# Weights of the first half in pairs of members, the later wait carried by the instruction, and two duties moved between engines

## The chip, the cores and the metric

The kernel runs on one core of a Trainium2 chip. TensorE (PE in the profile) multiplies matrices out of SBUF into PSUM, VectorE (DVE) and ScalarE (ACT) work elementwise, GpSimd (POOL) clears small tensors and issues gathers, and SyncE (SP) issues most of the transfers (DMAs). Each engine takes its own instructions in the order in which they are written; between engines there are only semaphores. The metric is the device time of one execution in microseconds. The kernel before takes 80.88 us, the median of three runs of 80.46, 80.88 and 80.88.

## The reference

```
w = weights[conditions]                       # x: 32 batches of 32 x 256, one 32 x 32 table entry per batch
y = einsum('bct,bcd->bdt', x, w)              # mixing
h = silu(y @ w_gate) * (y @ w_up)             # 256 -> 1024
h_sparse = keep the 2 largest |h| of every 4 neighbours, else 0
out = x + h_sparse @ w_down                   # 1024 -> 256
```

All numbers are 32-bit floats. The kernel gets their accuracy out of faster matmuls by dividing each operand into a high part (rounded) and a low part (what the rounding left), and adding three products: high by high, low by high, high by low.

## The kernel before

The 1024 rows of y are two halves of 512 (half 0 and 1). The 1024 columns of the gate and up matrices are two halves as well (q = 0 and 1), each of four members j = 0 to 3 of 128 columns: member j holds the columns that are j-th in their group of four, so the choice of 2 in 4 is elementwise among four tiles. A pair n is one gate product and one up product of 128 by 512 for one (half, q, j); there are 16 pairs, in the order half, q, j. Each product is 6 matmuls (three terms, two halves k of the 256 inputs). PSUM banks for pairs go round in threes.

The start, which the change touches, goes as follows. SP (L173 to L176) loads the condition numbers, x of half 0, and the k = 0 part of the q = 0 gate weights. POOL clears the tensor `warm` (L199) and marks blocks in `own_block` (L200 to L203). PE multiplies `warm` by itself 12 times (L520) while nothing else can be done. When the condition numbers are there, VectorE adds row numbers (L439), POOL gathers the table rows (L206), VectorE transposes them (L351) and spreads them on diagonals (L359); then PE mixes (L529 for k = 0, L543 for k = 1). ScalarE and VectorE divide each result y and each piece of the weights into high and low: ScalarE writes the high part (L233 weights, L237 y), VectorE subtracts it for the low part (L366 weights, L373 y). A piece of weights is one entry of the list `PIECES`; the semaphores `w_hi` and `w_lo` count pieces whose high and low part is there, `y_hi` and `y_lo` the same for y.

PE then computes the gates of pairs 0 and 1 side by side (`first_gates`, L570, 12 matmuls that alternate between the two pairs: for each k the terms high-high, low-high, high-low), after them the up products of pairs 0 and 1 (L558), pair 2, the mixing of half 1 (L543), and the pairs 3 to 15 (L558). Last come 102 matmuls by `w_down` (L600), the addition of x (L435) and six outputs, stored by SP (L194), the last of them by ScalarE's queue (L335).

An instruction can wait for several semaphores. The built program gives the wait that is written first to the instruction itself; those written after it become one instruction of their own ahead of it, which only waits. In the listings below, the last name in a bracket is the wait that the instruction carries, and the names ahead of it are those of the separate waiting instruction.

Of the kernel before, what the change touches and what calls it, by code (L numbers as in the profile page):

```python
# [5 lines left out]
NQ = 2  # L6
M = 4
# [3 lines left out]
def adaln_ffn(nc: bass.Bass, x: bass.AP, x_t: bass.AP, cond: bass.AP, table: bass.AP,  # L11
# [5 lines left out]
    f32 = mybir.dt.float32  # L17
    f32r = mybir.dt.float32r
    bf16 = mybir.dt.bfloat16
    ALU = mybir.AluOpType  # L20
# [27 lines left out]
    with ctx:  # L48
# [39 lines left out]
        y_banks = banks[:, 6:6 + KT]  # L88

        cond_in = sem("cond_in")  # L90
        x_in = [sem(f"x_in{i}") for i in range(NH)]
        w_in = [[None, sem("gate_in1")], [sem(f"up_in{q}") for q in range(NQ)]]
        first_in = [sem(f"first_in{k}") for k in range(KT)]
# [45 lines left out]
        def split_y(part, half, k, end):  # L139
# [6 lines left out]

        PIECES = [(0, w, k, k + 1) for w in range(2) for k in range(KT)] + \
                 [(q, w, 0, KT) for q in range(1, NQ) for w in range(2)]

        def pieces_until(q, w, k):  # L150
            return 1 + max(i for i, piece in enumerate(PIECES) if piece[:2] == (q, w) and piece[2] <= k)

        GATE_PIECES_END = PIECES.index((1, 0, 0, KT)) + 1

# [3 lines left out]
                   (1, 1, 0, TH // 2, gate_bank(PAIRS - 1)), (1, 1, TH // 2, TH, up_bank(PAIRS - 1))]  # L158
        UNFINISHED = 3
        HALVED = range(2, M)  # L160
# [5 lines left out]

        def raw_piece(q, w, k, end):

            return raw_w[w][:, q, k:end].rearrange("p k (j g) -> p k j g", j=M)

        @block.sync
        def _(sp):
            sp.dma_start(cond_sb[:], cond).then_inc(cond_in, 16)  # L173

            sp.dma_start(x_sb[:, 0:GH, :], x[0]).then_inc(x_in[0], 16)
            sp.dma_start(raw_w[0][:, 0, 0], w_gate[0, 0]).then_inc(first_in[0], 16)  # L176

            sp.wait_ge(mix_in[0], 16)
            for k in range(1, KT):
                sp.dma_start(raw_w[0][:, 0, k], w_gate[0, k]).then_inc(first_in[k], 16)  # L180
            sp.dma_start(raw_w[1][:, 0], w_up[0]).then_inc(w_in[1][0], 16)
            sp.wait_ge(w_in[1][0], 16)
            sp.dma_start(x_sb[:, GH:NG, :], x[1]).then_inc(x_in[1], 16)
            sp.dma_start(raw_w[0][:, 1], w_gate[1].rearrange("k p n -> p k n")).then_inc(w_in[0][1], 16)
            sp.dma_start(raw_w[1][:, 1], w_up[1]).then_inc(w_in[1][1], 16)
            sp.dma_start(down_raw[:], w_down).then_inc(down_in, 16)
            sp.wait_ge(w_hi, GATE_PIECES_END)
            sp.wait_ge(w_lo, GATE_PIECES_END)
            sp.dma_start(xt_sb, x_t).then_inc(xt_in, 16)
            for i, (half, k, begin, end, _) in enumerate(OUTPUTS[:-1]):  # L190
                if i != UNFINISHED:
                    cols = slice(half * TH + begin, half * TH + end)
                    sp.wait_ge(out_done, i + 1)
                    sp.dma_start(out[:, k, cols], xt_sb[:, k, cols]).then_inc(stored, 16)  # L194
            sp.wait_ge(stored, 16 * (len(OUTPUTS) - 1))

        @block.gpsimd
        def _(pool):
            nc.gpsimd.memset(warm[:], 0.0).then_inc(warm_zero, 1)  # L199
            nc.gpsimd.memset(own_block[:], 0.0).then_inc(blocks_marked, 1)  # L200
            pool.wait_ge(blocks_marked, 1)
            for b in range(NB):
                nc.gpsimd.memset(own_block[b * C:(b + 1) * C, b:b + 1], 1.0).then_inc(blocks_marked, 1)  # L203
            pool.wait_ge(rows_done, 1)
            for half in range(NH):
                nc.gpsimd.indirect_dma_start(  # L206
                    out=mix_row[:, half], out_offset=None, in_=table,
                    in_offset=bass.IndirectOffsetOnAxis(ap=rows_sb[:, half:half + 1], axis=0),
                    engine_sem=gather_sent,
                ).then_inc(mix_in[half], 16)  # L210

            def low_down(q):
                pool.wait_ge(down_neg, q + 1)
                pool.dma_start(down_hl[:, LO, q].rearrange("p j t -> p (j t)"), down_raw[:, q],  # L214
                               accum_op=ALU.add).then_inc(down_lo_sent[q], 16)

            def low_h(u, j, end):
                pool.wait_ge(h_neg, parts_until(u, j))
                pool.dma_start(h_hl[:, u, LO, j:end], hs[u][:, j:end],  # L219
                               accum_op=ALU.add).then_inc(h_lo_sent[u][j // 2], 16)  # L220

            low_down(0)
            low_down(1)
            for u in range(SENT):
                for j, end in PARTS[u]:
                    low_h(u, j, end)

        @block.scalar
        def _(act):

            def high_weights(q, w, k, end):
                act.wait_ge(first_in[k] if (q, w) == (0, 0) else w_in[w][q], 16)
                nc.scalar.activation(w_hl[w][:, HI, q, k:end], raw_piece(q, w, k, end), ACT.Copy).then_inc(w_hi, 1)  # L233

# [38 lines left out]
            for k in range(KT):  # L273
                high_weights(*PIECES[k])
                high_y(*Y_PIECES[k])
            for piece in PIECES[KT:2 * KT]:
                high_weights(*piece)
            act.wait_ge(table_loaded, 1)
            gate_silu(0)
            gate_silu(1)  # L280
            absolute(0)
            high_weights(*PIECES[4])
            gate_silu(2)
            absolute(1)
            high_weights(*PIECES[5])
            high_y(*Y_PIECES[KT])
# [44 lines left out]
            high_h(3, 3, 4)  # L331
            half, k, begin, end, _ = OUTPUTS[-1]
            cols = slice(half * TH + begin, half * TH + end)
            act.wait_ge(out_done, len(OUTPUTS))
            act.dma_start(out[:, k, cols], xt_sb[:, k, cols]).then_inc(stored, 16)  # L335

        @block.vector
        def _(dve):
# [23 lines left out]
            def low_weights(i):  # L362
                q, w, k, end = PIECES[i]
                dve.wait_ge(first_in[k] if (q, w) == (0, 0) else w_in[w][q], 16)
                dve.wait_ge(w_hi, i + 1)
                nc.vector.tensor_tensor(w_hl[w][:, LO, q, k:end], raw_piece(q, w, k, end),  # L366
                                        w_hl[w][:, HI, q, k:end].bitcast(f32), ALU.subtract).then_inc(w_lo, 1)

            def low_y(i):
                half, k, end = Y_PIECES[i]  # L370
                dve.wait_ge(mixed, KT * half + end)
                dve.wait_ge(y_hi, i + 1)
                nc.vector.tensor_tensor(split_y(LO, half, k, end), mixed_y(half, k, end),  # L373
                                        split_y(HI, half, k, end).bitcast(f32), ALU.subtract).then_inc(y_lo, 1)
# [54 lines left out]
            def output(i):  # L429
# [3 lines left out]
                if i > UNFINISHED:  # L433
                    dve.wait_ge(out_done, UNFINISHED + 1)
                nc.vector.tensor_tensor(xt_sb[:, k, cols], bank[:, begin:end], xt_sb[:, k, cols],  # L435
                                        ALU.add).then_inc(out_done, 1)

            dve.wait_ge(cond_in, 16)
            nc.vector.tensor_tensor(rows_sb[:], cond_sb[:, 0:NH], cond_sb[:, NH:2 * NH], ALU.add).then_inc(rows_done, 1)  # L439
            dve.wait_ge(blocks_marked, 1 + NB)  # L440
            transpose_rows(0)
            diagonal(SPANS[0])
            diagonal(SPANS[1])
            for k in range(KT):
                low_weights(k)
                low_y(k)
            for i in range(KT, 2 * KT):
                low_weights(i)
# [3 lines left out]
            diagonal(SPANS[2])  # L452
            low_weights(4)
            product(2)
            compare(0, 1)
            low_weights(5)
            low_y(KT)
# [59 lines left out]
        def _(pe):  # L517
# [4 lines left out]
            def mixing_by_batch():  # L522

                pe.wait_ge(x_in[0], 16)
                pe.wait_ge(transposed, 1)
                for g in range(GH):
# [22 lines left out]
            def split_product(dst, w, q, half, j):  # L549

                terms = [(s, m, k) for s, ms in ((HI, (HI, LO)), (LO, (HI,))) for k in range(KT) for m in ms]
                for i, (s, m, k) in enumerate(terms):

                    if half == 0 and j == 0:
                        pe.wait_ge(w_hi if s == HI else w_lo, pieces_until(q, w, k))
                    if q == 0 and j == 0:
# [5 lines left out]
            def first_gates():  # L562

                terms = [(s, m, k) for k in range(KT) for s, m in ((HI, HI), (LO, HI), (HI, LO))]
                for i, (s, m, k) in enumerate(terms):
                    if i > 0:
                        pe.wait_ge(w_hi if s == HI else w_lo, pieces_until(0, 0, k))
                    pe.wait_ge(y_hi if m == HI else y_lo, k + 1)
                    for n in (0, 1):
                        nc.tensor.matmul(gate_bank(n), w_hl[0][:, s, 0, k, n], y_hl[:, m, 0, k],  # L570
                                         start=i == 0, stop=i == len(terms) - 1)
# [35 lines left out]
            warm_up(WARM_START)  # L607
            pe.wait_ge(w_hi, pieces_until(0, 0, 0))
            mixing_by_batch()
# [64 lines left out]
```

## Time and profile before

| | us |
|---|---|
| runs | 80.46, 80.88, 80.88 (median 80.88) |
| profiled execution | 80.44 |
| its span, first to last instruction | 78.6 |
| busy: PE, PE weight loads, DVE, ACT, POOL | 74.5, 59.5, 62.1, 41.7, 8.6 |

The profile shows one execution; its span leaves 1.84 us of that execution's time outside. PE is busy for 95% of the span, so the time is PE's work, what stands ahead of it and behind it, and the short stretches in which PE's instructions do not follow each other at their own pace. Of a busy time on PE one should know that the end of a matmul is modelled; what counts is the distance from the start of one to the start of the next. The views below are the chain that ended last, tables of stretches (`--windows`: busy time and number of instructions of each engine, granted clock, share of the 16 DMA engines, GB/s) and timelines.

### The profile page before, as it was taken

What the parts mean: (1) busy time and instruction counts of PE and PEld (TensorE: products, weight loads), DVE (VectorE), ACT (ScalarE), POOL (GpSimd) and SP (SyncE); (2) the same over time, 40 slices, a digit from 0 to 9 for tenths busy, and PEclk for the clock granted to TensorE, in tenths of its full rate; (3) what the DMA queues carried; (4) which work ended last, traced back from release to release, by engine and by line L of the source; (5) the groups of instructions that cost most, each with busy time, mean ns of one, the idle gap of its engine ahead of it and who ended that gap; (6) DMA issues with size and microseconds to landing.
All of it is one profiled execution on the core that took longest, in us unless ns stands there. A gap on an engine that the chain in (4) does not pass through costs nothing.

```text
span 78.6 us, 1020 instructions
## 1 busy us (share of the span) xinstructions
PE 74.5 (95%) x362; PEld 59.5 (76%) x362; DVE 62.1 (79%) x91; ACT 41.7 (53%) x61; POOL 8.6 (11%) x18
## 2 busy tenths in 40 slices
PE   3999999999999999999999999999999999999950
PEld 1338778888888888888888888888888888888840
DVE  0017691699879999599999979999999999994460
ACT  6122753869453375599897769789380402730000
POOL 5550000000000013000713000006200000000000
PEclk9999999999999999999999999999999999999999
DMA  0857559984900004900099990003995000003333
GB/s 1 250 183 201 232 154 381 413 377 92 425 33 0 0 0 79 188 0 0 15 194 200 194 198 13 4 0 60 200 177 96 0 0 0 8 0 138 137 142 118
DMA packets 3221, 9.64 MB, mean 123 GB/s; under 512 B 496, under 2 KB 752, under 8 KB 2960
## 3 DMA queue, kind: packets, MB, share of 16 engines
q0 software_dynamic: 928, 3.28, 21.9%
q1 hardware_dynamic: 2144, 6.16, 21.8%
q10 hardware_dynamic: 144, 0.13, 0.5%
q8 instruction: 3, 0.05, 0.2%
q14 instruction: 2, 0.02, 0.1%
HBM read 5.38 MB, written 1.05 MB: 82 GB/s over the span
## 4 chain that ended last, share of the span: by engine, by line
PE 95%; POOL 1%; DVE 1%; issue 0%; POOLq 0%
PE banks L558 52%; PE banks L600 28%; PE banks L520 6%; PE banks L543 4%; PE banks L570 4%; PE banks L529 1%; POOL warm L199 1%; DVE gate_raw L435 1%; POOLq L663 0%
## 5 line engine op out<-in xcount | busy, mean ns | idle before, releaser
L558 PE MATMUL banks<-y_hl,up_hl 128*128 128x512 f32 x96 | 24.2, 389 | 0.0
L600 PE MATMUL banks<-h_hl,down_hl 128*128 128x512 f32 (+1 forms) x102 | 22.0, 376 | 0.0
L558 PE MATMUL banks<-y_hl,gate_hl 128*128 128x512 f32 x84 | 21.4, 390 | 0.0
L600 PEld LDWEIGHTS banks<-h_hl,down_hl 128*128 128x128 f32 x102 | 18.5, 188 | 3.6
L558 PEld LDWEIGHTS banks<-y_hl,up_hl 128*128 128x128 f32 x96 | 18.0, 188 | 3.8
L558 PEld LDWEIGHTS banks<-y_hl,gate_hl 128*128 128x128 f32 x84 | 15.7, 188 | 3.2
L243 ACT ACTIVATE silu<-banks 128x512 f32<-128x512 f32 x16 | 9.6, 597 | 12.4 <-PE banks L558 12.1
L384 DVE TENSOR_TENSOR h<-banks,silu 128x512 f32<-128x512 f32 x12 | 8.3, 689 | 4.4 <-ACT silu L243 4.4
L264 ACT ACTIVATE h_hl<-h 128x1024 fp32r<-128x1024 f32 (+1 forms) x8 | 6.7, 843 | 3.9 <-DVE h L420 3.9
L420 DVE SCALAR_TENSOR_TENSOR h<-count,h 128x512 f32<-128x512 bf16 x12 | 7.9, 687 | 0.1
L520 PE MATMUL banks<-warm 128*128 128x512 bf16 x12 | 4.8, 586 | 1.3 <-POOL warm L199 1.3
L250 ACT ACTIVATE x_sb<-h 128x512 f32<-128x512 f32 x8 | 4.9, 626 | 1.7 <-DVE h L384 1.7
L435 DVE TENSOR_TENSOR gate_raw<-banks,gate_raw 128x512 f32<-128x512 f32 (+1 forms) x6 | 3.5, 602 | 2.4 <-PE banks L600 2.3
L214 POOL DMA_DIRECT2D down_hl<-down_raw x2 | 1.8, 919 | 31.5 <-ACT down_hl L259 31.5
L219 POOL DMA_DIRECT2D h_hl<-h x4 | 3.7, 928 | 13.4 <-ACT h_hl L268 13.4
L395 DVE TENSOR_TENSOR far<-x_sb 128x1024 bf16<-128x1024 f32 x4 | 4.9, 1222 | 0.2
L395 DVE TENSOR_TENSOR far<-a_even 128x1024 bf16<-128x1024 f32 x4 | 4.9, 1220 | 0.2
L520 PEld LDWEIGHTS banks<-warm 128*128 128x128 bf16 x12 | 1.6, 141 | 4.1 <-issue 2.7
L268 ACT ACTIVATE h_hl<-h 128x1024 fp32r<-128x1024 f32 x4 | 4.2, 1054 | 0.0
L233 ACT ACTIVATE gate_hl<-gate_raw 128x512 fp32r<-128x512 f32 (+1 forms) x3 | 2.3, 771 | 3.6 <-DMA gate_raw<-in_w_gate 3.6
L264 ACT ACTIVATE h_hl<-up_raw 128x1024 fp32r<-128x1024 f32 x2 | 2.1, 1054 | 3.2 <-DVE up_raw L420 3.2
L351 DVE STREAM_TRANSPOSE h<-h 128x128 f32<-128x128 f32 x2 | 0.8, 406 | 3.1 <-DMA h<-in_table,rows_sb 3.1
(39 smaller groups left out, 68.1 us busy)
## 6 DMA issues: line engine op xcount, KB each, us to landing
h_hl<-h POOLq DMA_DIRECT2D x4, 512.0 KB, 6.1
x_sb<-in_x SPq DMA_DIRECT2D x2, 512.0 KB, 3.4
up_raw<-in_w_up SPq DMA_DIRECT2D x2, 512.0 KB, 4.7
down_raw<-in_w_down SPq DMA_DIRECT2D x1, 1024.0 KB, 7.8
gate_raw<-in_x_t SPq DMA_DIRECT2D x1, 1024.0 KB, 4.8
down_hl<-down_raw POOLq DMA_DIRECT2D x2, 512.0 KB, 5.0
out<-gate_raw SPq DMA_DIRECT2D x3, 256.0 KB, 2.4
gate_raw<-in_w_gate SPq DMA_DIRECT2D x2, 256.0 KB, 3.3
```

The costliest lines, as they stand in the source:

```text
L219: pool.dma_start(h_hl[:, u, LO, j:end], hs[u][:, j:end], accum_op=ALU.add).then_inc(h_lo_sent[u][j // 2], 16)
L243: nc.scalar.activation(silu[:, n % 3], gate_bank(n), ACT.Silu).then_inc(silu_done, 1)
L250: nc.scalar.activation(a[u % 2][:, j], hs[u][:, j], ACT.Abs).then_inc(abs_done, 1)
L264: nc.scalar.activation(h_hl[:, u, HI, j:end], hs[u][:, j:end], ACT.Copy).then_inc(h_hi, 1)
L268: nc.scalar.activation(h_hl[:, u, LO, j:end], hs[u][:, j:end], ACT.Copy, scale=-1.0).then_inc(h_neg, 1)
L384: nc.vector.tensor_tensor(hs[u][:, j], up_bank(n), silu[:, n % 3], ALU.mult).then_inc(h_done, 1)
L395: step(nc.vector.tensor_tensor(far[:, j - 2::2], au[:, 0:2], au[:, j:j + 1].broadcast_to([P, 2, TH]), ALU.is_ge))
L420: nc.vector.scalar_tensor_tensor(hs[u][:, j], count[:, j], bound, hs[u][:, j], op, ALU.mult).then_inc(masked, 1)
L435: nc.vector.tensor_tensor(xt_sb[:, k, cols], bank[:, begin:end], xt_sb[:, k, cols], ALU.add).then_inc(out_done, 1)
L520: nc.tensor.matmul(gate_bank(0), warm[:, 0:P], warm[:], start=True, stop=True)
L558: last = nc.tensor.matmul(dst, w_hl[w][:, s, q, k, j], y_hl[:, m, half, k], start=i == 0, stop=i == len(terms) - 1)
L600: last = nc.tensor.matmul(bank[:, begin:end], down_hl[:, s, q, j, k * P:(k + 1) * P], h_hl[:, u, m, j, begin:end], start=(q, j, m, s) == f ...
```

## The change

The q = 0 gate and up weights are no longer divided into pieces by k with all four members, but by pairs of members: the pieces are now gate k = 0 and gate k = 1 of members 0 and 1, up of members 0 and 1 (both k), then gate and up of members 2 and 3 (both k). The weights lie in HBM by pairs of members accordingly, so a partition's contiguous run in these transfers is 1 KB; the q = 1 weights come in two transfers each. Pair 2 waits for the new later pieces. Further, `warm` is cleared by VectorE; at many places the order in which two waits are written is exchanged; and the last of the six outputs is stored by SP, the one before it by ScalarE's queue.

```
+        PIECES = [(0, 0, k, k + 1, 0, 2) for k in range(KT)] + [(0, 1, 0, KT, 0, 2)] + \
+                 [(0, w, 0, KT, 2, M) for w in range(2)] + [(1, w, 0, KT, 0, M) for w in range(2)]
+        LATER = KT + 3
...
-        PIECES = [(0, w, k, k + 1) for w in range(2) for k in range(KT)] + \
-                 [(q, w, 0, KT) for q in range(1, NQ) for w in range(2)]
...
-        UNFINISHED = 3
+        UNFINISHED, LEFT = 3, 4
...
-            sp.dma_start(raw_w[0][:, 0, 0], w_gate[0, 0]).then_inc(first_in[0], 16)
+            sp.dma_start(raw_w[0][:, 0, 0, 0:2 * P], w_gate[0, 0, 0]).then_inc(first_in[0], 16)
 
             sp.wait_ge(mix_in[0], 16)
             for k in range(1, KT):
-                sp.dma_start(raw_w[0][:, 0, k], w_gate[0, k]).then_inc(first_in[k], 16)
-            sp.dma_start(raw_w[1][:, 0], w_up[0]).then_inc(w_in[1][0], 16)
-            sp.wait_ge(w_in[1][0], 16)
+                sp.dma_start(raw_w[0][:, 0, k, 0:2 * P], w_gate[0, 0, k]).then_inc(first_in[k], 16)
+            sp.dma_start(raw_w[1][:, 0, :, 0:2 * P], w_up[0, 0].rearrange("k p n -> p k n")).then_inc(up_in, 16)
+            for w, weights in enumerate((w_gate, w_up)):
+                sp.dma_start(raw_w[w][:, 0, :, 2 * P:4 * P],
+                             weights[0, 1].rearrange("k p n -> p k n")).then_inc(rest_in[w], 16)
+            sp.wait_ge(up_in, 16)
             sp.dma_start(x_sb[:, GH:NG, :], x[1]).then_inc(x_in[1], 16)
-            sp.dma_start(raw_w[0][:, 1], w_gate[1].rearrange("k p n -> p k n")).then_inc(w_in[0][1], 16)
-            sp.dma_start(raw_w[1][:, 1], w_up[1]).then_inc(w_in[1][1], 16)
+            for w, weights in enumerate((w_gate, w_up)):
+                for i in range(2):
+                    sp.dma_start(raw_w[w][:, 1, :, 2 * i * P:2 * (i + 1) * P],
+                                 weights[1, i].rearrange("k p n -> p k n")).then_inc(second_in[w], 16)
...
-            for i, (half, k, begin, end, _) in enumerate(OUTPUTS[:-1]):
-                if i != UNFINISHED:
+            for i, (half, k, begin, end, _) in enumerate(OUTPUTS):
+                if i not in (UNFINISHED, LEFT):
...
-            nc.gpsimd.memset(warm[:], 0.0).then_inc(warm_zero, 1)
             nc.gpsimd.memset(own_block[:], 0.0).then_inc(blocks_marked, 1)
...
-            half, k, begin, end, _ = OUTPUTS[-1]
+            half, k, begin, end, _ = OUTPUTS[LEFT]
...
+            nc.vector.memset(warm[:], 0.0).then_inc(warm_zero, 1)
             dve.wait_ge(cond_in, 16)
+            dve.wait_ge(blocks_marked, 1 + NB)
             nc.vector.tensor_tensor(rows_sb[:], cond_sb[:, 0:NH], cond_sb[:, NH:2 * NH], ALU.add).then_inc(rows_done, 1)
-            dve.wait_ge(blocks_marked, 1 + NB)
...
-                pe.wait_ge(x_in[0], 16)
                 pe.wait_ge(transposed, 1)
+                pe.wait_ge(x_in[0], 16)
...
-                    if half == 0 and j == 0:
-                        pe.wait_ge(w_hi if s == HI else w_lo, pieces_until(q, w, k))
+                    if half == 0 and (j == 0 or (q, j) == (0, 2)):
+                        pe.wait_ge(w_hi if s == HI else w_lo, pieces_until(q, w, k, j))
...
                 for i, (s, m, k) in enumerate(terms):
+                    pe.wait_ge(y_hi if m == HI else y_lo, k + 1)
                     if i > 0:
-                        pe.wait_ge(w_hi if s == HI else w_lo, pieces_until(0, 0, k))
-                    pe.wait_ge(y_hi if m == HI else y_lo, k + 1)
+                        pe.wait_ge(w_hi if s == HI else w_lo, pieces_until(0, 0, k, 0))
```

VectorE's first instructions in the kernel before, from the row numbers to the low parts of the q = 0 weights; `h` is the tensor in which the gathered and transposed table rows lie, `mix_in0` the arrival of the gather:

```order
L439 ISA rows_sb<-cond_sb 128x4 [waits cond_in]
L351 STREAM_TRANSPOSE h<-h 128x4x32 [waits mix_in0,blocks_marked]
L359 TENSOR_TENSOR h<-h,own_block 128x256 [waits transposed] x2
L366 TENSOR_TENSOR gate_hl<-gate_raw,gate_hl 128x512 [waits w_hi,first_in0]
L373 TENSOR_TENSOR y_hl<-banks,y_hl 128x512 [waits y_hi,mixed]
L366 TENSOR_TENSOR gate_hl<-gate_raw,gate_hl 128x512 [waits w_hi,first_in1]
L373 TENSOR_TENSOR y_hl<-banks,y_hl 128x512 [waits y_hi,mixed]
L366 TENSOR_TENSOR up_hl<-up_raw,up_hl 128x512 [waits w_hi,up_in0] x2
```

The same place in the changed kernel:

```order
L458 MEMSET warm 128x256
L461 ISA rows_sb<-cond_sb 128x4 [waits blocks_marked,cond_in]
L372 STREAM_TRANSPOSE h<-h 128x4x32 [waits mix_in0]
L380 TENSOR_TENSOR h<-h,own_block 128x256 [waits transposed] x2
L386 TENSOR_TENSOR gate_hl<-gate_raw,gate_hl 128x256 [waits first_in0,w_hi]
L393 TENSOR_TENSOR y_hl<-banks,y_hl 128x512 [waits mixed,y_hi]
L386 TENSOR_TENSOR gate_hl<-gate_raw,gate_hl 128x256 [waits first_in1,w_hi]
L393 TENSOR_TENSOR y_hl<-banks,y_hl 128x512 [waits mixed,y_hi]
L386 TENSOR_TENSOR up_hl<-up_raw,up_hl 128x2x256 [waits up_in,w_hi]
L386 TENSOR_TENSOR gate_hl<-gate_raw,gate_hl 128x2x256 [waits rest_in0,w_hi]
L386 TENSOR_TENSOR up_hl<-up_raw,up_hl 128x2x256 [waits rest_in1,w_hi]
```

The clearing of `warm` stands first; the transpose carries its only wait itself; the wait for ScalarE's high part (`w_hi`, `y_hi`) is now the one that each subtraction carries; the two gate pieces ahead of the y pieces are half as wide, and three pieces of 512 follow where two stood.

SP's transfers at the start of the kernel before:

```order
L175 DMA x_sb<-in_x 128x1024
L176 DMA gate_raw<-in_w_gate 128x512
L180 DMA gate_raw<-in_w_gate 128x512 [waits mix_in0]
L181 DMA up_raw<-in_w_up 128x1024
L183 DMA x_sb<-in_x 128x1024 [waits up_in0]
L184 DMA gate_raw<-in_w_gate 128x2x512
L185 DMA up_raw<-in_w_up 128x1024
L186 DMA down_raw<-in_w_down 128x2048
```

And in the changed kernel:

```order
L192 DMA x_sb<-in_x 128x1024
L193 DMA gate_raw<-in_w_gate 128x256
L197 DMA gate_raw<-in_w_gate 128x256 [waits mix_in0]
L198 DMA up_raw<-in_w_up 128x2x256
L200 DMA gate_raw<-in_w_gate 128x2x256
L200 DMA up_raw<-in_w_up 128x2x256
L203 DMA x_sb<-in_x 128x1024 [waits up_in]
L206 DMA gate_raw<-in_w_gate 128x2x256 x2
L206 DMA up_raw<-in_w_up 128x2x256 x2
L208 DMA down_raw<-in_w_down 128x2048
```

Ahead of SP's wait for the up weights stand four transfers instead of two; behind it six instead of four.

## Rows read from the trace of the kernel before

**Rows 1.** Chain that ended last: start us, us, what.
```profile
1.33 4.83 PE banks L520 x12
6.24 1.09 PE banks L529 x32
...
8.42 2.91 PE banks L570 x12
11.33 5.46 PE banks L558 x24
...
18.65 35.40 PE banks L558 x156
...
75.91 0.42 DVE gate_raw L435
```
**Rows 2.** Stretches: us, busy PE, PEld, DVE, ACT, POOL (count), PEclk, DMA, GB/s.
```profile
6.00:9.25 3.25, 3.17 (x46) 2.82 (x46) 2.23 (x6) 1.41 (x3) 0.00 (x0) 1.00 0.81 262
8.18:11.17 2.99, 2.99 (x16) 2.20 (x14) 2.60 (x5) 2.27 (x4) 0.00 (x0) 1.00 0.42 145
11.17:13.91 2.74, 2.74 (x14) 2.25 (x12) 0.99 (x2) 0.60 (x1) 0.00 (x0) 1.00 1.05 381
```
**Rows 3.** Timeline of the start: us, us, engine, line, operation, idle before.
```profile
0.75 0.52 POOL L199 MEMSET warm<- 128x512 bf16 x1 [0.29 <-POOLq L663]
...
2.41 0.16 DVE L439 CUSTOM_DVE_ANT_0 rows_sb<-cond_sb 128x4 uint16<-128x4 uint16 x1 [2.41 <-DMA cond_sb<-in_cond]
...
5.57 0.10 PEld L520 LDWEIGHTS banks<-warm 128*128 128x128 bf16 x1 [0.27 <-issue]
...
5.68 0.41 DVE L351 STREAM_TRANSPOSE h<-h 128x128 f32<-128x128 f32 x1 [3.11 <-DMA h<-in_table,rows_sb]
...
6.21 1.01 PEld L529 LDWEIGHTS banks<-h,x_sb 32*128 32x128 f32 x32 [0.54 <-ACT gate_hl L233]
...
7.39 0.60 ACT L237 ACTIVATE y_hl<-banks 128x512 fp32r<-128x512 f32 x1 [1.39 <-PE banks L529]
...
8.09 0.69 DVE L373 TENSOR_TENSOR y_hl<-banks,y_hl 128x512 fp32r<-128x512 f32 x1 [0.60 <-ACT y_hl L237]
...
8.44 0.63 ACT L233 ACTIVATE gate_hl<-gate_raw 128x512 fp32r<-128x512 f32 x1 [0.45 <-DMA gate_raw<-in_w_gate]
...
8.97 0.58 ACT L237 ACTIVATE y_hl<-banks 128x512 fp32r<-128x512 f32 x1
...
9.67 1.15 ACT L233 ACTIVATE up_hl<-up_raw 128x512 fp32r<-128x512 f32 x2
...
9.67 1.23 PEld L570 LDWEIGHTS banks<-y_hl,gate_hl 128*128 128x128 f32 x6 [0.29 <-issue]
...
12.81 0.60 ACT L243 ACTIVATE silu<-banks 128x512 f32<-128x512 f32 x1 [1.99 <-PE banks L558]
...
13.44 0.69 DVE L384 TENSOR_TENSOR h<-banks,silu 128x512 f32<-128x512 f32 x1 [1.75 <-ACT silu L243]
```
**Rows 4.** Last warm-up matmul, then PE's starts after 8.7 us (timeline, PE).
```profile
5.78 0.38 PE L520 MATMUL banks<-warm 128*128 128x512 bf16 x1
8.72 1.09 PE L570 MATMUL banks<-y_hl,gate_hl 128*128 128x512 f32 x4
```
**Rows 5.** Arrival of the two gathers after issue.
```profile
DMA to landing us min/median/max: 2.6/2.6/2.7
```
**Rows 6.** Transfers: KB each, median us from issue to landing.
```profile
out<-gate_raw SPq DMA_DIRECT2D x1, 128.0 KB, 1.9
out<-gate_raw ACTq DMA_DIRECT2D x1, 128.0 KB, 1.9
```
**Rows 7.** Timeline of the end.
```profile
74.48 1.22 DVE L435 TENSOR_TENSOR gate_raw<-banks,gate_raw 128x512 f32<-128x512 f32 x2 [0.67 <-PE banks L600]
...
75.73 0.33 SPq L194 DMA_DIRECT2D out<-gate_raw  x1
...
76.37 0.37 ACTq L335 DMA_DIRECT2D out<-gate_raw  x1
```

More of the change, by code:

```diff
@@ L88, in adaln_ffn, with pieces_until, source @@
         y_banks = banks[:, 6:6 + KT]
+        PIECES = [(0, 0, k, k + 1, 0, 2) for k in range(KT)] + [(0, 1, 0, KT, 0, 2)] + \
+                 [(0, w, 0, KT, 2, M) for w in range(2)] + [(1, w, 0, KT, 0, M) for w in range(2)]
+        LATER = KT + 3
+        def pieces_until(q, w, k, j):
+            return 1 + max(i for i, p in enumerate(PIECES) if p[:2] == (q, w) and p[2] <= k < p[3] and p[4] <= j < p[5])
+        def source(i):
+            q, w, k, _, j, _ = PIECES[i]
+            if q == 1:
+                return second_in[w], 32
+            if j == 2:
+                return rest_in[w], 16
+            return (first_in[k], 16) if w == 0 else (up_in, 16)
         cond_in = sem("cond_in")
         x_in = [sem(f"x_in{i}") for i in range(NH)]
-        w_in = [[None, sem("gate_in1")], [sem(f"up_in{q}") for q in range(NQ)]]
+        up_in = sem("up_in")
+        rest_in = [sem(f"rest_in{w}") for w in range(2)]
+        second_in = [sem(f"second_in{w}") for w in range(2)]
         first_in = [sem(f"first_in{k}") for k in range(KT)]
@@ L145, in adaln_ffn @@
         SPANS = [slice(0, 2), slice(2, 4), slice(4, 8)]
-        PIECES = [(0, w, k, k + 1) for w in range(2) for k in range(KT)] + \
-                 [(q, w, 0, KT) for q in range(1, NQ) for w in range(2)]
-        def pieces_until(q, w, k):
-            return 1 + max(i for i, piece in enumerate(PIECES) if piece[:2] == (q, w) and piece[2] <= k)
-        GATE_PIECES_END = PIECES.index((1, 0, 0, KT)) + 1
+        GATE_PIECES_END = PIECES.index((1, 0, 0, KT, 0, M)) + 1
         OUTPUTS = [(0, 0, 0, TH, y_banks[:, 0]), (0, 1, 0, TH, y_banks[:, 1]),
@@ L165, in parts_until, with raw_piece, split_piece @@
             return sum(len(p) for p in PARTS[:u]) + 1 + max(i for i, p in enumerate(PARTS[u]) if p[0] <= j)
-        def raw_piece(q, w, k, end):
-            return raw_w[w][:, q, k:end].rearrange("p k (j g) -> p k j g", j=M)
+        def raw_piece(i):
+            q, w, k, end, j, j_end = PIECES[i]
+            return raw_w[w][:, q, k:end].rearrange("p k (j g) -> p k j g", j=M)[:, :, j:j_end]
+        def split_piece(i, part):
+            q, w, k, end, j, j_end = PIECES[i]
+            return w_hl[w][:, part, q, k:end, j:j_end]
         @block.sync
@@ L229, in _, with high_weights @@
         def _(act):
-            def high_weights(q, w, k, end):
-                act.wait_ge(first_in[k] if (q, w) == (0, 0) else w_in[w][q], 16)
-                nc.scalar.activation(w_hl[w][:, HI, q, k:end], raw_piece(q, w, k, end), ACT.Copy).then_inc(w_hi, 1)
+            def high_weights(i):
+                act.wait_ge(*source(i))
+                nc.scalar.activation(split_piece(i, HI), raw_piece(i), ACT.Copy).then_inc(w_hi, 1)
             def high_y(half, k, end):
@@ L273, in _ @@
             for k in range(KT):
-                high_weights(*PIECES[k])
+                high_weights(k)
                 high_y(*Y_PIECES[k])
-            for piece in PIECES[KT:2 * KT]:
-                high_weights(*piece)
+            for i in range(KT, LATER):
+                high_weights(i)
             act.wait_ge(table_loaded, 1)
@@ L281, in _ @@
             absolute(0)
-            high_weights(*PIECES[4])
+            high_weights(LATER)
             gate_silu(2)
             absolute(1)
-            high_weights(*PIECES[5])
+            high_weights(LATER + 1)
             high_y(*Y_PIECES[KT])
@@ L362, in low_weights @@
             def low_weights(i):
-                q, w, k, end = PIECES[i]
-                dve.wait_ge(first_in[k] if (q, w) == (0, 0) else w_in[w][q], 16)
                 dve.wait_ge(w_hi, i + 1)
-                nc.vector.tensor_tensor(w_hl[w][:, LO, q, k:end], raw_piece(q, w, k, end),
-                                        w_hl[w][:, HI, q, k:end].bitcast(f32), ALU.subtract).then_inc(w_lo, 1)
+                dve.wait_ge(*source(i))
+                nc.vector.tensor_tensor(split_piece(i, LO), raw_piece(i),
+                                        split_piece(i, HI).bitcast(f32), ALU.subtract).then_inc(w_lo, 1)
             def low_y(i):
                 half, k, end = Y_PIECES[i]
+                dve.wait_ge(y_hi, i + 1)
                 dve.wait_ge(mixed, KT * half + end)
-                dve.wait_ge(y_hi, i + 1)
                 nc.vector.tensor_tensor(split_y(LO, half, k, end), mixed_y(half, k, end),
@@ L446, in _ @@
                 low_y(k)
-            for i in range(KT, 2 * KT):
+            for i in range(KT, LATER):
                 low_weights(i)
@@ L452, in _ @@
             diagonal(SPANS[2])
-            low_weights(4)
+            low_weights(LATER)
             product(2)
             compare(0, 1)
-            low_weights(5)
+            low_weights(LATER + 1)
             low_y(KT)
@@ L522, in mixing_by_batch @@
             def mixing_by_batch():
+                pe.wait_ge(transposed, 1)
                 pe.wait_ge(x_in[0], 16)
-                pe.wait_ge(transposed, 1)
                 for g in range(GH):
@@ L607, in _ @@
             warm_up(WARM_START)
-            pe.wait_ge(w_hi, pieces_until(0, 0, 0))
+            pe.wait_ge(w_hi, pieces_until(0, 0, 0, 0))
             mixing_by_batch()
@@ L649, in columns @@
         w = _np.asarray(w).reshape(T // P, P, NQ, P, M)
-        return w.transpose(2, 1, 0, 4, 3).reshape(NQ, P, T // P, M * P)
+        return w.transpose(2, 4, 0, 1, 3).reshape(NQ, 2, M // 2, T // P, P, P).transpose(0, 1, 3, 4, 2, 5).reshape(
+            NQ, 2, T // P, P, -1)
     down = _np.asarray(inputs["L0_ffn_w_down"]).reshape(NQ, P, M * T).transpose(1, 0, 2)
@@ L657 @@
         "table": table,
-        "w_gate": columns(inputs["L0_ffn_w_gate"]).transpose(0, 2, 1, 3),
+        "w_gate": columns(inputs["L0_ffn_w_gate"]),
         "w_up": columns(inputs["L0_ffn_w_up"]),
```

2 lines of the change are left out of this document (1 added, 1 removed).

## The prediction, made before the changed kernel was run

> **What bounds the kernel now.** I read the chain that ended last first, because with PE busy for 95% of the span the question is which stretches of PE are not run at its own pace. The chain is PE from 1.33 us on, and VectorE and a store at the end [rows 1]. From 11.33 us PE runs at 5.46 / 24 = 0.2275 us per matmul of 512 columns, and the 156 after 18.65 us at 35.40 / 156 = 0.227. Nothing there waits, so no wait that goes there can pay. Three places are left: what stands ahead of the mixing at 6.24, the first gates, and the end behind PE.
>
> Ahead of the mixing the timeline [rows 3] shows what was late. The gather wakes the transpose at 5.68; it ends at 6.09; PE's first weight load for the mixing starts at 6.21, 0.12 later. The page blames ScalarE's gate piece for that wait, but the transpose ended last of what the rows show. The twelve warm-up matmuls were just over. The weights of the twelfth were loaded at 5.57, when the eleventh starts, and (5.57 - 1.33) / 10 = 0.424 is the lower level of the clock (512 columns at 1.2 GHz are 0.427); the twelfth starts at 5.78 [rows 4], 0.21 later, which is the higher level. At that pace it gives PE free at 5.99, 0.22 before the load. The column of the granted clock reads 1.00 throughout [rows 2], so the level is read from the spacing alone.
>
> The first gates are 12 matmuls from 8.18 to 11.17, 2.99 us; the next 12 take 2.74 [rows 2]. So 0.25 us are lost. The third matmul starts at 8.72 [rows 4] instead of 8.18 + 2 x 0.228 = 8.64: 0.08 is lost there, just behind the wait for the first y. The rest, 0.17, is lost around 9.67, where the weight load had been idle for 0.29 and starts 0.12 after ScalarE's second y (8.97 + 0.58 = 9.55) [rows 3]. That y is late because ScalarE was at the k = 1 gate piece from 8.44 to 9.07, and that piece was late because its 256 KB were.
>
> **The change part by part.** The sum is made against the profiled execution's 80.44 us, 0.5% below the median of 80.88.
>
> Order of waits. Hand-overs of both kinds stand in the trace. Where the late wait is carried by a waiting instruction of its own, VectorE starts 0.10 after ScalarE's end (7.39 + 0.60 = 7.99 to 8.09). Where the instruction carries it, 0.03 (12.81 + 0.60 = 13.41 to 13.44) [rows 3]. So one exchange is worth 0.07 where it is on the path. On the path is the transpose, whose wait for the gather the instruction now carries: -0.07, of which I take 0.06, since this releaser is a transfer. PE's own first load keeps the transpose in the separate wait, because the w_hi wait is still written first: 0. The row addition gets a second wait, for the marked blocks, but the marking has no duty at 2.41 us and moves earlier with POOL's 0.52 us of clearing gone: 0. VectorE's subtractions for y and weights get 0.07 each; those of y feed the third term of each k, hidden behind the first two: 0 on their own.
>
> Less traffic ahead of the gather. The first gate transfer is 128 KB instead of 256. The two gathers arrive 2.6 and 2.7 us after issue [rows 5], the second after the x and first gate transfers have ended. So this is worth 0 to 0.1; I take 0.05, the middle, because the rows do not say which of the two gathers is the late one.
>
> The half as wide gate pieces. The 0.17 around 9.67 goes if the second y is ready 0.2 us earlier. With 256 columns for 512, the k = 1 high part costs between 0.32 (half of 0.63) and 0.63. If the transfer came no earlier than before, it would run from 8.44 to 8.76 at best, and y from there to 9.37: 0.18 earlier. The transfer has half its bytes; at the mean rate of that stretch, 262 GB/s [rows 2], 131 kB are 0.5 us. Then ScalarE goes to the piece straight from the first y (7.93 in the new times), ends by 8.56 even at the full 0.63, and the second y is there by about 9.0 to 9.2. The stall is gone then: -0.17, bounds -0.08 (no earlier arrival) and -0.25 (all of the loss). The 0.08 behind the first y stays, since nothing there changes.
>
> Warm-up cleared by VectorE. POOL needs 0.52 from 0.75 on [rows 3]. VectorE's clearing of 128 x 256 is not in the trace; the nearest rows are 0.16 (128 x 4) and 0.69 (128 x 512). So the warm-up starts between 0.17 later and 0.36 earlier; I take half of the 0.69 for half the width, 0.35, so 0.17 earlier. In this execution that is worth nothing: PE was free 0.22 before the transpose let it go, which covers the later case as well but for 0.01 to 0.02. It has a price only where PE is not free by then, which is the second case below.
>
> Rest pieces and more transfers. Members 2 and 3 add a transfer and a piece each for gate and up. Pair 2 needs them 12 matmuls after the first gates, near 13.7; I expect the transfers by about 10 to 11 and the divisions, 0.6 to 0.7 each, by 12.5. ScalarE idled 1.99 before 12.81 [rows 3], which is the cover. SP issues two transfers more before its wait for the up weights, but that wait ends earlier with half the bytes: 0. The Trainium skill, page "DMA: Bandwidth & Descriptors", section "Bandwidth", speaks against this edit: it wants transfers batched to 1 MiB or more. By that rule the pieces of 128 and 256 KB would lose rate. The rows have 262 GB/s over pieces of 256 and 512 KB; what slower ones would do is the last case below.
>
> Last store. ScalarE's queue issued it 0.04 after VectorE's end (75.91 + 0.42 = 76.33 to 76.37), SP issued the one before 0.03 after (75.70 to 75.73) [rows 1, 7], and both kinds take 1.9 us [rows 6]: 0, bounds -0.05 and +0.05.
>
> Sum: -0.06 - 0.05 - 0.17 = -0.28. PE's later stages move as a block, since ScalarE and VectorE follow PE there. 80.44 - 0.28 = 80.16, a factor of 0.9965; on the median, 80.88 x 0.9965 = 80.60. By the bounds of its terms (0 to -0.07, 0 to -0.10, -0.08 to -0.25, and 0.05 either way for the store) the change is worth -0.03 to -0.47 in this execution, 80.41 to 80.85 on the median.
>
> **The rivals.**
>
> More than the profile shows. The shown runs lie at 80.46 and at 80.88, and the profiled one at 80.44 is of the quicker kind. If in the others the clock rises later, the warm-up's last matmuls run at 0.427 each and PE is not free until 1.33 + 12 x 0.427 = 6.45, 0.24 after the transpose. There the earlier start of the warm-up pays its 0.17 of that 0.24, beside the 0.28: 80.88 - 0.45 = 80.43, and less if the mixing too leaves the lower level earlier. For it: two of three runs lie 0.42 higher, and 0.24 plus some mixing at the lower level would make that. Against it: no row shows such a run. The Trainium skill, page "TensorE: Matmul & The Clock Gate", says that the moment of the rise differs by half a microsecond between runs of one kernel; no run shown here can confirm it. With 5.57 moved by that much it would be this case by estimate.
>
> It does not do what it says. If the transfer of the k = 1 gates is ruled by its fixed time and not by its bytes, and the gather does not come earlier, then only 0.06 to 0.14 is left: about 80.8.
>
> Slower by the transfers. Four transfers of 1 KB runs must land before ScalarE can go on to the first silu, at 12.81 - 0.28 = 12.53. The last of them, the up weights of members 2 and 3, must be there 0.63 earlier, at 11.9. From 6.0 on they and the second gather are 983 kB; with some 0.6 for arrival (the row of 6.00 to 9.25 ends its bytes there, and the up weights were used at 9.67 after a landing just before) this needs 983 kB / 5.3 us = 185 GB/s, against 262 so far. If runs of 1 KB halve the rate to 131, the last bytes come at 13.5 and the piece at 14.1, 2.2 late. Silu 0, silu 1 and the diagonals of half 1 follow in order on ScalarE and VectorE. I count half of the 2.2 as hidden, because silu 1 itself came 1.3 after silu 0 and only then the diagonals: +1.1 - 0.28 = +0.8, 81.7. Against it: the change halves a partition's run for the gates and quarters it for the up weights, and less than a third of the rate may go before anything waits.
>
> **How the numbers follow.** The forecast 0.48, more than that 0.34, no effect 0.10, slower transfers 0.08. A measurement of this kernel tells no change from about 0.5%, 0.40 us. Of the forecast 0.15 lies beyond that, of the second case 0.9, of the third none: faster 0.07 + 0.31 = 0.38. Slower: the last case and 0.01 for what nobody saw, 0.09. The rest, 0.53, is within. The range 80.0 to 81.1 holds the first three cases, with 0.4 below the second for what the mixing may gain, and leaves out most of the last.
>
> **What would show it.** PE's first mixing load at about 6.1 instead of 6.21; the transpose 0.03 to 0.07 after the gather; ScalarE's k = 1 gate piece right behind the first y, at about 7.9; no idle weight load near 9.5; 12 first gates in about 2.8 us; the tail behind PE unchanged; PE at 0.227 per matmul from then on. It would be wrong if PE waits at pair 2 or at the mixing of half 1, if the k = 1 gates land at 8.4 as before, or if the mixing runs at the lower level after a longer idle of PE.

## The result, and the profile after

Six runs of the changed kernel took 80.18 to 80.35 us, median 80.21; six of the kernel before, beside them, 80.46 to 80.88, median 80.75. The ratio is 0.9943, with a 95% interval of 0.992 to 0.9967. A second comparison, of twelve runs against 33, gave 0.9965 (0.9949 to 0.9982), which is the forecast's factor. The ratios here are estimates over all runs of a comparison, not quotients of the two medians (0.9933 in the first), and runs more than 1.5% above the fastest of their kernel are not counted in them. The profiled execution took 80.31 us, its span 78.4.

The chain that ended last, of the changed kernel (start us, us, what), answers to [rows 1]:

```profile
1.20 4.46 PE banks L541 x12
5.66 0.57 issue
6.23 1.09 PE banks L550 x32
...
8.41 2.73 PE banks L591 x12
11.14 5.44 PE banks L579 x24
...
18.44 35.39 PE banks L579 x156
...
75.69 0.42 DVE gate_raw L455
```

The last addition comes 0.22 us earlier (75.91 to 75.69), and PE's pace behind the first gates is what it was (35.39 for 156). The mixing starts where it did, 6.23 for 6.24; nearly all of this execution's gain, 0.19, is made in the first gates (8.41 to 11.14, before 8.42 to 11.33). The warm-up ended 0.50 earlier, and PE then waits 0.57 with nothing to do. Of the 0.50, 0.13 is the earlier start of the warm-up; the rest is that it lasted 4.46 instead of 4.83, because the clock rose earlier in this execution.

The stretches of the first gates and the 12 matmuls behind them, columns as in [rows 2]:

```profile
8.16:10.98 2.82, 2.82 (x15) 2.35 (x14) 2.53 (x5) 2.27 (x5) 0.00 (x0) 1.00 0.85 240
10.98:13.70 2.72, 2.72 (x13) 2.25 (x12) 1.56 (x3) 0.98 (x2) 0.00 (x0) 1.00 0.98 322
```

The first gates lose 0.10 now, 0.25 before. The timeline of the start, to be held against [rows 3]:

```profile
0.87 0.27 DVE L458 MEMSET warm<- 128x256 uint32 x1 [0.87 <-PEq L685]
...
2.53 0.16 DVE L461 CUSTOM_DVE_ANT_0 rows_sb<-cond_sb 128x4 uint16<-128x4 uint16 x1 [1.39 <-DMA cond_sb<-in_cond]
...
5.72 0.33 SPq L197 DMA_DIRECT2D gate_raw<-in_w_gate  x1
5.72 0.40 DVE L372 STREAM_TRANSPOSE h<-h 128x128 f32<-128x128 f32 x1 [3.03 <-DMA h<-in_table,rows_sb]
...
6.20 1.01 PEld L550 LDWEIGHTS banks<-h,x_sb 32*128 32x128 f32 x32 [1.03 <-ACT gate_hl L254]
...
7.38 0.60 ACT L258 ACTIVATE y_hl<-banks 128x512 fp32r<-128x512 f32 x1 [1.96 <-PE banks L550]
7.89 0.42 ACT L254 ACTIVATE gate_hl<-gate_raw 128x256 fp32r<-128x256 f32 x1
8.01 0.69 DVE L393 TENSOR_TENSOR y_hl<-banks,y_hl 128x512 fp32r<-128x512 f32 x1 [0.75 <-ACT y_hl L258]
8.14 2.58 PEld L591 LDWEIGHTS banks<-y_hl,gate_hl 128*128 128x128 f32 x12
...
8.45 0.60 ACT L258 ACTIVATE y_hl<-banks 128x512 fp32r<-128x512 f32 x1
```

Four things are to be seen. The condition numbers came 0.12 later in this execution (2.53 for 2.41), so the gather was issued 0.13 later too (2.99 for 2.86), and what the waits give is spent on that. SP and the transpose, which both wait for the gather alone, start together at 5.72. ScalarE takes the k = 1 gate piece at 7.89 right behind the first y. And the twelve weight loads of the first gates merge into one row from 8.14, with no idle time in it; before, they stood in two rows with 0.29 between.

### The profile page after: what moved, and what is told of

It is laid out like the page before. It is cut to its first block, busy times and chain, and to the rows that moved or that the text cites. A ratio compares the mean times of both kernels' runs of the same rounds, so it can differ in the third digit from the quotient of the medians.

```text
span 78.4 us, 1027 instructions
## 1 busy us (share of the span) xinstructions
PE 73.9 (94%) x362; PEld 59.6 (76%) x362; DVE 62.7 (80%) x93; ACT 42.1 (54%) x62; POOL 8.1 (10%) x17
## 4 chain that ended last, share of the span: by engine, by line
PE 94%; issue 1%; DVE 1%
PE banks L579 52%; PE banks L621 28%; PE banks L541 6%; PE banks L564 4%; PE banks L591 3%; PE banks L550 1%; DVE gate_raw L455 1%; DVE warm L458 0%
## 5 line engine op out<-in xcount | busy, mean ns | idle before, releaser
L254 ACT ACTIVATE gate_hl<-gate_raw 128x256 fp32r<-128x256 f32 (+2 forms) x4 | 2.5, 632 | 3.2 <-DMA gate_raw<-in_w_gate 3.1
L258 ACT ACTIVATE y_hl<-banks 128x512 fp32r<-128x512 f32 (+1 forms) x3 | 2.2, 737 | 2.1 <-PE banks L550 2.0
```

## The experiments

After the result the theories were these. First, the forecast's own: the halved gate pieces close the gap in the first gates, the waits give the transpose 0.06. Second, the prediction's larger case: executions of the kernel before near 80.9 are those whose clock rises late, so that the warm-up ends after the transpose. Third: they are those whose gather is held up by the first gate transfer. A clock that rises late is one that is still at the lower of TensorE's two levels (1.2 GHz, 0.427 us per matmul of 512 columns) at the end of the warm-up. All comparisons are of 12 runs (13 in one) against 35 of the kernel before on the same chip; in the comparison of "Each edit left out" two of the 35 took 97.41 and 265.81 us, and 33 count. To compare spreads I count runs more than 0.4 us above a kernel's lowest; of the kernel before these are 38 of 103.

### Each edit alone

Pieces alone (the changed kernel with the other edits undone):

```
-        PIECES = [(0, w, k, k + 1) for w in range(2) for k in range(KT)] + \
-                 [(q, w, 0, KT) for q in range(1, NQ) for w in range(2)]
+        PIECES = [(0, 0, k, k + 1, 0, 2) for k in range(KT)] + [(0, 1, 0, KT, 0, 2)] + \
+                 [(0, w, 0, KT, 2, M) for w in range(2)] + [(1, w, 0, KT, 0, M) for w in range(2)]
```

> Weights by pairs of members alone; waits, clearing and last store as before. Theory 1 (the half as wide gate pieces close the gap in the first gates): the 12 first gates take about 2.82 instead of 2.99 us, PE's end moves by 0.17 to 0.22, median ratio 0.997 to 0.998, spread of the runs still about 0.4 us. Theory 2 (the runs at 80.88 are those in which the warm-up ends too late, and the earlier clearing removes them): as theory 1 here, and the high runs stay. Theory 3 (the high runs are those in which the gather is held up by the first gate transfer, whose bytes are halved): median ratio 0.994 to 0.996 and no runs more than 0.25 above the lowest.

Ratio 1.0005 (0.9987 to 1.0023), runs 80.39 to 80.93. The third theory falls: the spread stays. The gap is closed in the profile, 2.76 for the first gates in its chain (2.91 before), with the mixing at 6.26. The median did not move, so the 0.997 to 0.998 of the first theory was missed too; the interval lies above it.

Clearing alone:

```
-            nc.gpsimd.memset(warm[:], 0.0).then_inc(warm_zero, 1)
+            nc.vector.memset(warm[:], 0.0).then_inc(warm_zero, 1)
```

> VectorE clears the warm-up tensor, nothing else. Theory 1: PE starts about 0.1 to 0.15 us earlier, the mixing does not, ratio 0.999 to 1.001. Theory 2: the lowest run stays near 80.45, the high runs go, median near 80.5, ratio 0.995 to 0.997. Theory 3: ratio 1.000, runs still between 80.45 and 80.9.

Ratio 1.0004 (0.9988 to 1.002), runs 80.48 to 80.75. The high runs went, as the second theory wants, but no run came below 80.48 either, and the median did not move. In its profile the gather had come late: the transpose ran from 5.93, so the mixing started at 6.48 although the warm-up was over at 5.89. So this run, of 80.64, was held up by the gather and not by the clock. Whether a late gather is also what kept the other eleven runs at 80.48 or above is not shown.

Waits alone (five places; two of them):

```
-                pe.wait_ge(x_in[0], 16)
                 pe.wait_ge(transposed, 1)
+                pe.wait_ge(x_in[0], 16)
...
-            dve.wait_ge(blocks_marked, 1 + NB)
```

> Only the order of the waits is exchanged. Theory 1: the transpose starts 0.04 to 0.07 after the gather's arrival instead of 0.13 and PE's mixing 0.06 earlier; VectorE's subtractions start 0.03 after ScalarE instead of 0.10; ratio 0.999. Rival: the handovers get no shorter, or the transpose gains and the row addition loses the same by its second wait; ratio 1.000.

Ratio 0.9987 (0.9964 to 1.0011), runs 80.14 to 81.01. This is the widest spread of the four single edits, with a lowest run below all of the kernel before (80.25); the interval includes 1. Its timeline:

```profile
5.61 0.33 SPq L180 DMA_DIRECT2D gate_raw<-in_w_gate  x1
5.62 0.41 DVE L351 STREAM_TRANSPOSE h<-h 128x128 f32<-128x128 f32 x1 [3.06 <-DMA h<-in_table,rows_sb]
...
6.09 1.01 PEld L529 LDWEIGHTS banks<-h,x_sb 32*128 32x128 f32 x32 [1.12 <-ACT gate_hl L233]
```

The transpose starts 0.01 behind SP. PE's load follows it by 6.09 - 6.03 = 0.06, where it was 0.12 [rows 3], though on PE only the two names inside the separate waiting instruction changed places.

Last store alone:

```
-            for i, (half, k, begin, end, _) in enumerate(OUTPUTS[:-1]):
-                if i != UNFINISHED:
+            for i, (half, k, begin, end, _) in enumerate(OUTPUTS):
+                if i not in (UNFINISHED, LEFT):
```

> The last store comes from SP, the one before it from ScalarE. All theories so far: ratio 1.000 within 0.001, the end after PE's last matmul 2.7 us as before. Rival: stores from SP end sooner or later than those from ScalarE in the device time outside the span; then ratio 0.998 or 1.002.

Ratio 1.0002 (0.9985 to 1.0019): the store is worth nothing. The profile, though, was of an execution of 80.86 us, the kind that no trace had shown. Its chain, then its timeline:

```profile
1.33 5.30 PE banks L520 x12
6.63 1.34 PE banks L529 x32
...
9.06 2.75 PE banks L570 x12
```
```profile
5.57 0.15 PEld L520 LDWEIGHTS banks<-warm 128*128 128x128 bf16 x1 [0.27 <-issue]
...
5.73 0.41 DVE L351 STREAM_TRANSPOSE h<-h 128x128 f32<-128x128 f32 x1 [3.17 <-DMA h<-in_table,rows_sb]
...
6.56 1.30 PEld L529 LDWEIGHTS banks<-h,x_sb 32*128 32x128 f32 x32 [0.84 <-ACT gate_hl L233]
```

The load at 5.57 takes 0.15 here and took 0.10 in [rows 3]: the clock had not risen. (The column of the granted clock reads 1.00 in this trace as well, so the level is read from the rows.) The warm-up lasts 5.30 instead of 4.83. The transpose was done at 6.14, PE's load came at 6.56, 0.42 behind it, and the mixing took 1.34 for 1.09. Beside the profiled execution of the kernel before, the mixing starts 0.39 later in the chain (6.63 for 6.24) and lasts 0.25 longer, and the first gates take 0.16 less (2.75 for 2.91): 0.48 in the sum, for 0.42 between the two times (80.86 and 80.44). That is the mechanism of the second theory, in a trace.

From here the theory was a fourth: the mixing starts at the last of two independent arrivals, the warm-up's end and the gather's chain, both of which move by some tenths from run to run; behind it the first gates have a gap only if the mixing was early. How far the clock moves is seen in the length of the twelve warm-up matmuls, 4.14 us in the trace of the waits alone and 5.30 in this one. So one edit moves one arrival and mostly meets the other.

### Each edit left out

The changed kernel again, unaltered:

> The changed kernel once more, beside the three that leave one edit out. Theory 4 (the mixing starts at the last of three arrivals: the warm-up's end, the gather's chain, and behind it the first gates at the later of PE's pace and ScalarE's k = 1 chain; so single edits give nothing and all together give more than their sum): ratio 0.993 to 0.996, runs within 0.25 us of each other. Rival (additive: the four single edits measured 1.0005, 1.0004, 0.9987 and 1.0002, which add up to nothing, and the first comparison was drift): ratio 0.998 to 1.001.

Ratio 0.9965 (0.9949 to 0.9982), runs 80.18 to 80.67, nine of twelve below 80.35. The gain is no drift, though the spread is wider than the 0.25 that was expected. The profile was of the run of 80.57, and in it both arrivals were late: SP's wait for the gather ended 3.09 after POOL's issue (5.94 - 2.85), 2.74 in the kernel before, and the warm-up lasted 5.17. The transpose was done at 6.35, the mixing started at 6.46 and took its usual 1.09.

POOL clears again:

```
-            nc.vector.memset(warm[:], 0.0).then_inc(warm_zero, 1)
+            nc.gpsimd.memset(warm[:], 0.0).then_inc(warm_zero, 1)
```

> POOL clears the warm-up tensor again, all else as changed. Theory 4: in executions whose clock rises late the warm-up ends last again, at about 6.45 us, so the high runs come back; lowest run as in the changed kernel (80.2), highest 80.6 or more, median ratio 0.996 to 0.998. Rival (the clearing is hidden): like all edits together, ratio 0.994, narrow.

Ratio 1.0024 (1.0002 to 1.0046), median 80.79, lowest 80.16, eight of twelve at 80.69 to 81.01. The direction is the fourth theory's and the size is more than it said: it does not explain a ratio above 1, and with twelve runs I leave open whether late rises were only frequent by chance. Its profile was of the 80.16 execution: mixing at 6.06 and first gates in 2.73, the early end of both arrivals.

Old order of waits (the edit of the waits above, undone in the changed kernel):

> The waits in the old order, all else as changed. Theory 4: the gather's chain is what ends last when the warm-up is early, so its 0.07 us return: transposed 0.13 us after the gather, mixing 0.06 later, ratio 0.995 to 0.996. Rival (waits are worth most, as the single runs hint with 0.9987): ratio 0.997 to 0.999.

Ratio 0.9984 (0.9963 to 1.0004), median 80.47 against 80.26: by the medians the waits are worth 0.2, more than the 0.07 that I gave them, but the intervals of the two kernels overlap and the size is not settled. In its profile the transpose ended at 6.24 and PE's load came at 6.35, 0.11 later, the long hand-over again.

Pieces by k again (the edit of the pieces above, undone in the changed kernel):

> Weights by k with all four members again, all else as changed. Theory 4: the gap of about 0.17 us in the first gates is back, also the larger first transfer ahead of the gather: 12 first gates in 2.95 to 3.0 us, ratio 0.996 to 0.998. Rival (the pieces are worth nothing, as alone): ratio as all edits together.

Ratio 0.9993 (0.9974 to 1.0011), lowest run 80.36 against 80.18. So beside the other edits the pieces are worth about 0.0028 of the time, 0.2 us (the two intervals just touch), and alone nothing that was measured. Its profile shows an execution in which they are worth nothing. The chain:

```profile
1.20 5.30 PE banks L520 x12
6.50 1.02 PE banks L529 x32
...
8.62 2.75 PE banks L570 x12
```

Here the clock rose late, the mixing was late, and the undivided k = 1 gates were ready in time: 2.75, no gap, where 2.95 to 3.0 was expected. The other traces agree, but for the one of 83.80 us below. From the start of the first gates to the start of the next matmuls, undivided gates took 2.98 and 2.99 us where the mixing started at 6.12 and 6.24, and 2.83 to 2.87 in the four traces where it started between 6.43 and 6.56; halved gates took 2.82 to 2.85 in seven traces, with the mixing anywhere from 6.06 to 6.46. That the runs which lose by the undivided gates are the lowest ones, those with an early mixing, follows from this and fits the lowest run of 80.36.

### The warm-up's length and PE's wait

The kernel before with one warm-up matmul less:

```
-    WARM_START = 12
+    WARM_START = 11
```

> The kernel before with 11 instead of 12 warm-up matmuls. Theory 4 (in executions whose clock rises late, the warm-up's end starts the mixing): the twelfth matmul's 0.43 us at the lower level is what those executions lose, so the runs above 80.65 become fewer than the third to two fifths seen of the kernel before; lowest run unchanged at 80.3 to 80.45; median ratio 0.997 to 0.999. Rival (the runs differ by when the transfers arrive, not by the clock): same spread and ratio 1.000 as before. Second rival (the shorter warm-up moves the clock's rise behind the mixing): ratio 1.002 or more.

Ratio 0.999 (0.9966 to 1.0015). Of the nine runs that it counts, one lies above 80.65, but three more took 81.96, 83.86 and 83.88 us. Four of twelve are then high, beside 17 of 35 of the kernel before, so it is not shown that high runs became fewer, as theory four had it: the three may be those that would have been high. The second rival, that the clock rises behind the mixing, fits them, at a price far above what it said; none of the three was traced.

The changed kernel with 11:

> The changed kernel with 11 warm-up matmuls. Theory 4: the warm-up already ends before the transpose in most executions, so ratio within 0.001 of the changed kernel's 0.9943 to 0.9965, and fewer runs above 80.45. Second rival (as above): 0.998 or more.

Ratio 0.9957 (0.9937 to 0.9978), and again three runs beside it, of 81.99, 83.77 and 83.82 us.

PE's wait for the transpose written first of three, so that the mixing's first matmul carries it:

```
-            pe.wait_ge(w_hi, pieces_until(0, 0, 0, 0))
             mixing_by_batch()
...
                 pe.wait_ge(transposed, 1)
                 pe.wait_ge(x_in[0], 16)
+                pe.wait_ge(w_hi, pieces_until(0, 0, 0, 0))
```

> The changed kernel with the wait for the transpose written first on PE, so that the mixing's first matmul carries it and the wait for the high part goes to the separate instruction. Theory 4: the load follows the transpose by about 0.05 instead of 0.08 to 0.12 and the mixing comes 0.04 to 0.07 earlier wherever the transpose ends last: lowest runs near 80.12, ratio 0.9935 to 0.996. Rival: PE's hand-over is the same either way, ratio as the changed kernel.

Ratio 0.9959 (0.9933 to 0.9985), lowest 80.06. It cannot be told from the changed kernel's. Its profile was of the 80.83 execution, with the late clock: the transpose is done at 6.01, and PE's load comes at 6.43. Its chain:

```profile
1.20 5.30 PE banks L541 x12
6.50 1.32 PE banks L551 x32
```

So the earlier clearing has not made the late kind impossible, only 0.13 cheaper at that place: 6.43 for the 6.56 above.

Both together:

> Both together. Theory 4: lowest runs near 80.12 and few above 80.4, ratio 0.993 to 0.9955, the best so far. Second rival: as all edits or slower, 0.997.

Ratio 0.9957 (0.9936 to 0.9978), lowest 80.04, two of 13 at 81.92 and 83.80 us. The profile is of the latter. Its chain and the two rows of its timeline ahead of the mixing:

```profile
6.24 1.93 PE banks L551 x32
8.17 2.00 PE banks L565 x8
10.18 4.54 PE banks L592 x12
14.72 5.44 PE banks L580 x24
```
```profile
5.78 0.40 DVE L372 STREAM_TRANSPOSE h<-h 128x128 f32<-128x128 f32 x1 [3.13 <-DMA h<-in_table,rows_sb]
...
6.24 1.79 PEld L551 LDWEIGHTS banks<-h,x_sb 32*128 32x128 f32 x32 [1.07 <-DVE h L372]
```

The load follows the transpose (done at 6.18) by 0.06, no better than with the two names exchanged: the rival on the hand-over holds as far as one trace goes. PE was idle for 0.17 ahead of the mixing, and mixing and first gates then ran at the lower level for most of their time, by their pace; the column of the granted clock reads 1.00 here too (the mixing's 32 matmuls 1.93 instead of 1.09, the first gates 4.54 / 12 = 0.378 each, between the 0.427 and 0.227 of the two levels): 8.48 us for what takes 4.91 in the changed kernel (6.23 to 11.14), 3.6 us more. What set the lower level off is open, and the idle time alone does not tell the runs apart: in the traces of the two other kernels with 11 matmuls PE was idle for longer, and the mixing took its 1.09:

```profile
6.47 1.09 PE L529 MATMUL banks<-h,x_sb 32*128 32x32 f32 x32 [0.27 <-DVE h L351]
```
```profile
6.25 1.09 PE L550 MATMUL banks<-h,x_sb 32*128 32x32 f32 x32 [0.85 <-DVE h L372]
```

The first is the kernel before with 11, the second the changed kernel with 11. Eleven matmuls are no better version.

## Why the prediction was right, point by point

**First gates.** The step held to the hundredth: 2.99 to 2.82, -0.17, by the path that it named (the k = 1 piece at 7.89, forecast 7.93; the second y done at 9.05, forecast 9.0 to 9.2). What it did not say is that this gain exists only in executions whose mixing is early: the profiled one, with the mixing at 6.24, was such a case.

**Waits.** The transpose's hand-over: before, it started 0.08 behind SP, which waits for the same gather and issued at 5.60 before; after, with it. So -0.08 for the -0.06 taken. "PE's own first load keeps the transpose in the separate wait: 0" was wrong by 0.05: over the profiled executions in which the transpose came last, the load followed it by 0.11 to 0.12 in four traces with the old order and by 0.06 to 0.08 in those with the new.

**Less traffic ahead of the gather.** Not seen. From POOL's issue of the gather to SP's next transfer, which waits for it, six traces with 256 KB in the first gate transfer took 2.70 to 2.99, eight with 128 KB 2.70 to 3.09; the arrival moves by 0.4 between executions and not with the bytes. The 0.05 should have been 0.

**Clearing.** 0.27 on VectorE, but from 0.87 and not 0.75, so the warm-up starts 0.13 earlier for the 0.17 taken. In the profiled execution it was hidden, as forecast: PE idled 0.57.

**Store and rest pieces.** The store 0, by its own run. The rest pieces came in time: ScalarE still idled 1.25 ahead of the first silu.

**Sum.** -0.28 forecast, and 0.22 in the chain of the profiled execution, whose condition numbers were 0.12 late; between the two profiled times it is 0.13 (80.44 to 80.31), since the time outside the span grew from 1.84 to 1.91. That the sum came near is partly luck: the 0.05 for less traffic was too much, and the waits were given about 0.07 too little. The base was luck of the other kind. On the median 80.60 was forecast and 80.21 measured, but 80.88 was the median of three runs, and that of 103 is 80.56; the factor 0.9965 of this is 80.28, beside the 80.26 of the second comparison.

The second comparison has the forecast's 0.9965; the first has 0.9943, 0.54 us between the medians, and its runs of the kernel before held three of six at 80.88. The larger gain is the case that the prediction gave 0.34. Its mechanism, the late clock, is in the traces of a run of 80.86 and one of 80.83, with the mixing at its lower pace; the prediction had PE free there at 6.45 (0.24 behind the profiled execution's load at 6.21, and not behind the transpose, as it says), and the load came at 6.56. That the earlier clearing makes such runs rarer is a count: over 0.4 above the lowest run lie 20 of 48 runs of kernels with POOL's clearing (beside 38 of 103 of the kernel before) and 9 of 66 with VectorE's, 12 warm-up matmuls in each. The count does not say which of these runs had the late clock. The forecast and this case are not rivals: both shares can be in every comparison, in changing parts.

**The slower rival.** Transfers of 1 KB runs did not bind: the up weights of members 2 and 3 were taken at 10.72, with 11.9 as the bound.

## What to carry to other kernels

Where a stage starts at the last of several arrivals that each vary from run to run, price an edit against the arrivals' spread and test it beside the others; alone, three edits here measured nothing that, left out singly, cost 0.2 to 0.5 us between the medians. Write first the wait that ends last: on VectorE a wait carried by the instruction handed over 0.07 us sooner than one ahead of it (0.03 for 0.10); on PE the order inside the separate wait counted 0.05, and carrying the wait gave no more in the one trace of it. Where the executions of one kernel differ by more than the effect, a median of few runs is in part a draw; ask for the trace of a slower one before explaining it.

## What the runs showed of the hardware that was not expected

One warm-up matmul less, 0.43 us at the lower level, left 29 of 37 executions where they were and cost the others 1.5 to 3.6 us. In the one of these that was traced PE was idle for 0.17 us ahead of the mixing, which then ran at the lower level; in two of the unharmed it was idle for 0.27 and 0.85 us. So what decides is not shown. None of the 12-matmul kernels of the study showed this in 66 runs with the earlier clearing, even with PE idle for 0.57 us in one trace.
